# Cross-attention with LayerNorm: rows with every key masked are marked per tile from the row maximum, not per batch from a minimum over the mask

## The reference

```
qs = (x @ wq) by heads;  ks = (ctx @ wk);  vs = (ctx @ wv)
scores = qs ks^T / sqrt(32)
scores = where(mask, -inf, scores)
attn   = softmax(scores) @ vs
out    = attn @ wo + x
y      = (out - mean) / sqrt(var + 1e-5) * gamma + beta
```

## Time and profile before

| what | value |
|---|---|
| time, median of 3 runs | 631.47 us (631.15 to 632.55) |
| time of the profiled execution | 630.17 us |
| its span | 628.4 us |
| mean granted TensorE clock | 0.998 of full speed |
| busy: PE / DVE / ACT / POOL | 602.3 / 518.0 / 501.2 / 491.8 us |
| instructions: PE / DVE / ACT / POOL | 3820 / 995 / 1546 / 639 |

### The profile page before, as it was taken

One profiled execution on the slowest core, in us unless ns is written; L12 is line 12 of the kernel. 1 busy time (PEld: TensorE's weight loads), 2 busy tenths in 40 slices (PEclk: granted clock), 3 DMA queues, 4 the chain that ended last, 5 costly groups with the idle time before them and its releaser, 6 DMA issues.

```text
span 628.4 us, 12817 instructions
## 1 busy us (share of the span) xinstructions
PE 602.3 (96%) x3820; PEld 471.4 (75%) x3820; DVE 518.0 (82%) x995; ACT 501.2 (80%) x1546; POOL 491.8 (78%) x639
## 2 busy tenths in 40 slices
PE   7998999999899999999999999999999999998995
PEld 5776686887768788787868878787876878786763
DVE  3487687988779888888879888888888888888887
ACT  4578887888878888888978888898987888786851
POOL 4477459797968979797996979798896979687784
PEclk9999999999999999999999999999999999999999
DMA  8528365564554745454474645465453545643103
GB/s 291 190 48 205 96 162 151 167 166 130 145 179 118 188 131 154 137 168 134 127 200 125 162 136 167 135 160 161 136 167 94 168 142 146 209 110 102 51 34 118
DMA packets 61716, 91.30 MB, mean 145 GB/s; under 512 B 18384, under 2 KB 19408, under 8 KB 61648
## 3 DMA queue, kind: packets, MB, share of 16 engines
q1 hardware_dynamic: 61648, 90.49, 50.5%
HBM read 39.53 MB, written 16.78 MB: 90 GB/s over the span
## 4 chain that ended last, share of the span: by engine, by line
PE 66%; DVE 9%; SPq 7%; ACT 6%; POOL 5%; DMA 3%; issue 3%; POOLq 0%; DVEq 0%; ACTq 0%
PE bank L398 22%; PE bank L494 19%; PE bank L444 6%; PE bank L434 5%; PE bank L428 4%; ACT pr L607 4%; PE bank L467 3%; SPq L296 2%; PE bank L448 2%; SPq L264 2%; DVE pr L743 2%; PE bank L472 2%; PE bank L376 2%; SPq L271 2%; DVE nm L749 1%
## 5 line engine op out<-in xcount | busy, mean ns | idle before, releaser
L607 ACT ACTIVATE pr<-pr,nm 128x77 f32<-128x77 f32 x1024 | 270.0, 349 | 44.8 <-DVE nm L749 43.0
L905 POOL TENSOR_TENSOR pn<-pr,rec 128x512 f32<-128x512 f32 x128 | 135.1, 1056 | 86.9 <-DVE rec L758 82.8
L743 DVE SCALAR_TENSOR_TENSOR pr<-msk,bank 128x308 f32<-128x308 uint8 x256 | 109.8, 469 | 38.3 <-PE bank L434 33.1
L756 DVE TENSOR_REDUCE sm<-pr 128x8 f32<-128x616 f32 x128 | 99.8, 780 | 8.8 <-ACT pr L607 7.7
L398 PE MATMUL bank<-xh,wqh 128*128 128x512 f32 x256 | 104.7, 409 | 2.3 <-DVE ql L731 2.3
L494 PE MATMUL bank<-woh,ah 128*128 128x512 f32 x256 | 104.0, 406 | 1.4 <-DVE al L765 1.4
L749 DVE TENSOR_REDUCE nm<-pr 128x8 f32<-128x616 f32 x128 | 101.8, 795 | 4.4
L574 ACT ACTIVATE ptr<-bank 128x512 f32<-128x512 f32 (+1 forms) x256 | 95.7, 428 | 9.5 <-PE bank L444 9.4
L494 PE MATMUL bank<-woh,al 128*128 128x512 f32 x256 | 101.2, 395 | 0.0
L494 PE MATMUL bank<-wol,ah 128*128 128x512 f32 x256 | 101.1, 395 | 0.0
L398 PE MATMUL bank<-xh,wql 128*128 128x512 f32 x256 | 101.0, 394 | 0.0
(11 more groups left out here) (73 smaller groups left out, 974.2 us busy)
## 6 DMA issues: line engine op xcount, KB each, us to landing
qd<-qn SPq DMA_DIRECT2D x240, 128.0 KB, 2.5
xraw<-xT SPq DMA_DIRECT2D x58, 256.0 KB, 3.4
xres<-x SPq DMA_DIRECT2D x58, 256.0 KB, 2.9
out<-y SPq DMA_DIRECT2D x56, 256.0 KB, 2.0
ptr<-xT SPq DMA_DIRECT2D x6, 256.0 KB, 8.9
zt<-x SPq DMA_DIRECT2D x6, 256.0 KB, 4.2
out<-zt SPq DMA_DIRECT2D x6, 256.0 KB, 2.0
wk_sb<-wk SPq DMA_DIRECT2D x4, 256.0 KB, 4.8
```

The lines of the kernel that those rows point to most:

```text
L607: last = nc.scalar.activation(s, s, ACT.Exp, bias=nm[:, t % 2, h:h + 1], scale=1.0)
L743: nc.vector.scalar_tensor_tensor(out=pr[:, 4 * g:4 * g + 4, :], in0=msk[:, b % 2, t % TB, :].unsqueeze(1).broadcast_to([P, 4, LK]), scalar ...
L756: nc.vector.tensor_reduce(sm[:, t % 2, hs], pr[:, hs, :], AX.X, ALU.add).then_inc(v_sum, 1)
L905: nc.gpsimd.tensor_tensor(pn[:, half, 0:4, :].rearrange("p s (e k) -> p (s e) k", e=2), pr[:, hs, 0:KM], rec[:, t % 2, hs].unsqueeze(2).br ...
```

## The change

`mask_all` and its buffer `pf` (128 bytes to a partition) go. In their place `mark_masked(t)`, one DVE instruction for each of the 64 tiles, multiplies the negated row maximum of the tile's first head by 1.2 and then by 0. For an ordinary row that is 0. For a row with every key masked the negated maximum is about 3e38, the first product overflows, and the second makes NaN of it. In the loop it stands at the end of each tile; for the last four tiles it stands behind `row_sums(t, 0)` or, for the last, behind `row_sums(T-1, 1)`. The semaphore `v_ps` counts tiles now, not batches: GpSimd's `deviation(o)` waits for `o + 1`, and the mask load no longer waits for it.

```
-            def mask_all(b):
-                ts = slice(b * TB, (b + 1) * TB)
-                nc.vector.tensor_reduce(pf[:, 0], msk[:, b % 2], AX.X, ALU.min).then_inc(v_pf, 1)
-                dve.wait_ge(v_pf, 2 * b + 1)
-                nc.vector.tensor_scalar(pf[:, 1], pf[:, 0], MASKED, 10.0, ALU.mult, ALU.mult).then_inc(v_pf, 1)
-                dve.wait_ge(v_pf, 2 * b + 2)
-                nc.vector.tensor_tensor(poison[:, ts], pf[:, 1], pf[:, 1], ALU.subtract).then_inc(v_ps, 1)
+            def mark_masked(t):
+
+                dve.wait_ge(v_max, 2 * t + 1)
+                nc.vector.tensor_scalar(poison[:, t:t + 1], nm[:, t % 2, 0:1], 1.2, 0.0, ALU.mult, ALU.mult).then_inc(v_ps, 1)
...
-                if t % TB == 1:
-                    mask_all(t // TB)
+                mark_masked(t)
...
             row_sums(T - 4, 0)
+            mark_masked(T - 4)
             residual(T - 10)
...
             row_sums(T - 3, 0)
+            mark_masked(T - 3)
             residual(T - 8)
...
             row_sums(T - 2, 0)
+            mark_masked(T - 2)
             residual(T - 7)
...
             row_sums(T - 1, 1)
+            mark_masked(T - 1)
             residual(T - 4)
...
                 if b >= 2:
                     sp.wait_ge(v_st, NG * TB * (b - 1))
-                    sp.wait_ge(v_ps, b - 1)
...
             def deviation(o):
                 e = slot(o)
-                pool.wait_ge(v_ps, o // TB + 1)
+                pool.wait_ge(v_ps, o + 1)
```

More of the change, by code:

```diff
@@ L91, in cross_attention_layernorm @@
         poison = sb("poison", [P, T])
-        pf = sb("pf", [P, 2, TB])
         gam = sb("gam", [P, D])
@@ L181, in cross_attention_layernorm @@
             sem(n) for n in ("a_w", "a_k", "a_v", "a_xh", "a_qh", "a_pt", "a_exp", "a_ah", "a_ap"))
-        v_z, v_w, v_k, v_pf, v_ps, v_ql, v_st, v_max, v_sum, v_rec, v_al, v_res, v_bs, v_bn, v_y = (
-            sem(n) for n in ("v_z", "v_w", "v_k", "v_pf", "v_ps", "v_ql", "v_st", "v_max", "v_sum", "v_rec",
+        v_z, v_w, v_k, v_ps, v_ql, v_st, v_max, v_sum, v_rec, v_al, v_res, v_bs, v_bn, v_y = (
+            sem(n) for n in ("v_z", "v_w", "v_k", "v_ps", "v_ql", "v_st", "v_max", "v_sum", "v_rec",
                              "v_al", "v_res", "v_bs", "v_bn", "v_y"))
```

## The result

The changed kernel took 627.08 us (median of six runs, 624.94 to 628.83) beside 631.24 us for the kernel before (six runs, 629.92 to 632.55): ratio 0.9937, 95% interval 0.9916 to 0.9958. In a second comparison, on another occasion, it took 626.28 us (12 runs) beside 629.52 us (35 runs): 0.9952, 0.9932 to 0.9972. It is faster, by 0.5 to 0.6%.

The account below looks back on a forecast made before the run. PE was taken to bound the kernel through most of tiles 6 to 59, so only its waits cost time. Removing mask_all -3.0 us, tail marks +0.24 us: -2.8 us, from 631.47 to 628.7 us; range 627.5 to 631.3 us.

Parts of the forecast that it names:

- The three stalls: Behind tiles 17, 33 and 49 PE waits for ql because mask_all holds DVE; removal saves 3.0 us.
- The cover: In tiles 4n+1 DVE can be held about 0.8 us (0.09 + 0.74) before PE's projection waits for ql.
- The hold of `mask_all`: At the end of tile 17 mask_all delays DVE's next sm by 1.78 us, 1.0 us above what PE tolerates.
- The marks: 64 added 128x1 DVE instructions, 0.12 us each; free for PE in the loop, +0.24 us in the tail.
- the tail: Last tiles, where DVE is itself on the path: marks 59 and 62 add 0.12 us each, +0.24 us.
- DVE's idle before the second `mask_max`: In the other three tiles of a block, DVE's wait for PE's scores would shrink by 0.1 us.
- its own spread: The forecast case's span, 627.9 to 629.6 us, for mark cost and differences between runs.
- A held mark: GpSimd holds the added DVE instruction in tiles 4n+1; at 1.4 us each, +8.2 us, 639.7 us; chance 0.09.
- Given back at the batch ends: PE waits longer for qd transfers at batch ends, returning the 3.0 us; 630.7 to 631.7 us; chance 0.11.
- The change doesn't do what it says: The stall behind tiles 17, 33 and 49 belongs to the new batch and stays; 631.7 us; chance 0.05.

Follow-up runs that it names:

- e3: The kernel before with mask_all of batches 1 to 3 moved within tiles 17, 33 and 49 to before the first low_a half, no marks; 628.04 us, ratio 0.9968.
- e4: The changed kernel, layout of before, plus one idle DVE reduction of 8 mask rows in each of 14 tiles 4n+1; 627.7 us, ratio 0.9951.
- e2: The changed kernel with neither mask_all nor marks, the marks' buffer zeroed once at the start; 625.86 us, ratio 0.9946.
- e1: The changed kernel with the unused 128 bytes of pf kept, so later buffers lie as before; 627.06 us, ratio 0.9962.
- h1: The changed kernel with marks of 128x2 in place of 128x1; 627.2 us, ratio 0.9966.
- g2: The changed kernel with 128 unused bytes behind xh and xl, so only buffers behind them lie as before; 627.12 us, ratio 0.9950.

## Why the prediction was right or wrong

*The three stalls: right.* They were priced at 1.01, 1.01 and 0.99 us; with the layout equal they are worth 1.02 us each. They go because DVE is held for less than the cover (`e3`, `e4`), not because DVE has less work: `e2` takes all marks out and gains nothing.

*The cover: right in kind, and its agreement partly luck.* It was put at about 0.8 us, counted up to PE's start; it is 0.67 us, since PE starts 0.06 us behind the end of `ql` and the 0.09 us of idle are not part of it once the hold is measured by how much later `sm` starts. The hold of `mask_all` was put at 1.78 us, counted from the start of its reduction, and is 1.61 us. Above the cover there are 0.06 us of a slower second matmul as well. The three errors cancel: 1.78 - 0.8 and 1.61 - 0.67 + 0.06 both give 1.0 us, the agreement that the forecast called its base.

*The marks: mis-sized.* 0.12 us each in the tail, 0.24 us in all, was the price of an instruction behind which the next starts 0.10 to 0.12 us later. Where DVE doesn't wait for another engine, the next one starts 0.01 to 0.04 us behind the start of a mark, and the tail shows nothing. The forecast that DVE's busy time would rise by 4 us fell with it: it is 514.2 us, 3.8 us less, and 511.2 us in `e2`, so 64 marks add 3.0 us. Nor did DVE's idle before the second `mask_max` shrink: its waits for PE's scores are 34.8 us in 46 times, where they were 33.1 us in 42.

*The step that failed: the sum had no term for the layout.* The forecast counted instructions, waits and transfers; that the change also takes out 128 bytes and moves every buffer behind them, it put at nothing. From tile 17's product with V to the end of the span the traces take 447.9 and 448.4 us before, 445.4 us in `e1`, and 444.5 and 444.0 us in the changed kernel: 2.7 us for the instructions and 1.2 us for the layout, 0.1 us in each block of four tiles. Before tile 17 the spread hides it. With this term, and without the 0.24 us of the tail, the sum is -3.06 - 1.2 = -4.3 us and 627.2 us, where 627.08 us was measured. The traces show the missing piece; the timed runs don't resolve it. The forecast's ratio of 0.9956 lies inside both intervals, and the second comparison gave 3.2 us, so a part of the distance to 627.08 us may be the spread of the runs.

*The range.* Its lower end of 627.5 us follows from no row: the lowest sum that the prediction works out is -3.0 us, 628.5 us, and its own spread ended at 627.9 us. The median of before alone moved from 631.24 to 629.52 us between two comparisons, and the changed kernel's own runs spread over 4 us.

*The rivals.* A held mark: the mechanism is there (`e3`, `h1`), but not for one element, and not above the cover in this place. Given back at the batch ends: not behind tile 17; the steps from tile 29 to 33 and from 45 to 49 take 36.23 and 36.65, 36.35 and 37.11 us in the traces of before, and 36.31 and 37.01, 36.24 and 36.54 us in those of the changed kernel; they differ between runs of either kernel by as much as between the two. The change doesn't do what it says: `e3` rules it out.

## What to carry to other kernels

A lump of work on an engine off the path costs nothing up to a cover that can be read as the time between its last output and the start of the matmul that wants it, less what lies between them when the matmul does wait (0.06 us here); above it the excess counts. The same work in pieces below the cover is free, or in a gap of the same tile. A change that takes a buffer away moves all buffers behind it: before a gain of a few tenths of a per cent is put down to instructions, run the changed kernel with the old layout.

## What the runs showed of the hardware that was not expected

A float32 `tensor_scalar` on DVE within SBUF with 2 or 16 elements to a partition waits for a GpSimd product that is running: 0.70 us for 0.18 us, ending 0.03 us behind it (`e3`). Of the five marks of `h1` that began within 0.02 us of the product's start, four were not held (0.14 us). With one element it does not wait: 64 marks of 0.10 to 0.15 us. The Trainium skill, page SBUF - State Buffer, section "Who interferes with whom", names the lock on the shared ports, and page VectorE: DVE Perf Modes, section "What auto-detection actually checks", ties the two-port mode to one source and a destination in SBUF whose outermost dimensions other than one are both even or equal. Both agree with these rows: two and sixteen elements are even, and one element has no such dimension.

The place of `xh`, `xl` and the buffers behind them within 256 bytes changes the matmuls of the Q projection by 3 to 4 ns of 393 (the changed kernel beside `e1`); the place of `xh` and `xl` alone by 1 to 2 ns (`g2`).

The granted clock of PE fell after a wait in some runs and not in others, in either kernel. The changed kernel's PE around 173 us (idle before it in brackets), and busy times with the granted clock (the third column from the right) in the same stretch of the changed kernel and of the second trace of before:

```profile
173.51 0.45 PE L432 MATMUL bank<-kd,qd 128*128 128x154 f32 x2 [2.69 <-DMA qd<-qn]
...
175.45 0.63 PE L396 MATMUL bank<-xh,wqh 128*128 128x512 f32 x1
175.87 0.63 PE L396 MATMUL bank<-xl,wqh 128*128 128x512 f32 x1
```
```profile
171.50:180.00 8.50, 6.49 (x28) 5.39 (x29) 5.72 (x13) 5.09 (x18) 5.77 (x8) 0.80 0.46 161
```
```profile
172.00:180.00 8.00, 7.57 (x32) 6.28 (x33) 6.73 (x13) 4.89 (x15) 5.94 (x10) 0.79 0.55 173
```

Matmuls 0.42 us apart in place of 0.23 are the lower level, 1.2 GHz, for some of that stretch; PE had idled for 2.69 us before. The step from tile 13 to 17 takes 40.34 us here and 39.80 us in that trace of before, and 38.19 us in its first, where PE idled for 2.05 us and the clock stayed. The length of the idle does not decide it: before the fall in the second trace of before it was 2.08 us, and in `e1` PE idled for 2.50 us and the clock stayed. In the traces the stretch before tile 17 holds most of the spread: its product with V starts between 179.1 and 182.5 us over the 14 of them.
